# Expert loop of a mixture-of-experts kernel: outputs in two PSUM banks in turns, turned activations in one

## The chip, the core and the metric

The kernel runs on one core of a Trainium2 chip. A core has a matrix engine (TensorE, PE in the profile, with its weight loads as PEld), a vector engine (VectorE, DVE), a scalar engine (ScalarE, ACT), a general engine (GpSimd, POOL) and a queue for transfers (SyncE, SP). Results of TensorE land in PSUM, which this kernel uses as eight banks of 128 x 512 fp32. Each engine works through its own instructions in order; semaphores tie them together. The metric is the device time of one execution in microseconds (us); less is better.

## What is computed

A block of a transformer: a mixture-of-experts layer at half weight, attention, and the same mixture-of-experts layer again, on 4096 tokens of width 128. All arithmetic is fp32. The change lies in the mixture-of-experts layer, which runs twice:

```python
def _L0_ffn_ref(hidden_states, router_w, gate_w, up_w, down_w):
    B, S, H, F, E, TOPK = (4, 256, 128, 512, 8, 2)
    ...
    router_logits = x @ router_w.T
    top_vals, top_idx = jax.lax.top_k(router_logits, TOPK)
    routing_weights = jax.nn.softmax(top_vals, axis=-1)
    combine = jnp.sum(jax.nn.one_hot(top_idx, E, dtype=x.dtype) * routing_weights[..., None], axis=1)
    out = jnp.zeros_like(x)
    for e in range(E):
        g = x @ gate_w[e].T
        u = x @ up_w[e].T
        y = jax.nn.silu(g) * u @ down_w[e].T
        out = out + combine[:, e:e + 1] * y
    return out.reshape(b, s, h)

x = x + 0.5 * _L0_ffn_ref(_layernorm(x, axis=-1), ...)
x = x + _L0_attn_ref(_layernorm(x, axis=-1), L0_attn_W_qkv, L0_attn_W_out)
x = x + 0.5 * _L0_ffn_ref(_layernorm(x, axis=-1), ...)
```

## The kernel before

Three stages follow each other: `ffn` (f1), `attention`, `ffn` (f2). In `ffn` a first part normalizes the tokens, writes them to DRAM, routes them and sorts the 8192 token-expert pairs by expert into 72 blocks of 128 rows (`BLOCKS`), each block of one expert. The second part is the expert loop, the place of the change. A third part reads the results back and adds them with their weights.

In the expert loop the work for a block is spread over several iterations, so that one iteration j holds pieces of different blocks:

- POOL gathers the rows of block j+4 from DRAM (`gather`, L201, into one of four tiles `xb`), once PE has turned block j, and then scatters the output of block j-3 to DRAM (`scatter`, L593, from one of four tiles `y`), once ACT has copied it there. Both are indirect DMAs that POOL issues itself.
- PE, in this order: `turn_hidden(j-2)` turns the hidden activations of block j-2 (four transposes, L631); `turn_rows(j+1)` turns the gathered rows of block j+1 (L613); `project_down(j-3)` multiplies the turned activations of block j-3 with the down weights (L639, four matmuls in fp32, which the profile shows as eight records); `project(j)` does the gate and up projections of block j (L622 to L624, twice).
- ACT: copies the turned activations of block j-2 to `hidT` (L671), the turned rows of block j+1 to `xt` (L677), the output of block j-3 to `y` (L683), and makes silu of the gate of block j (L687).
- DVE: subtracts the rounded rows from the exact ones for block j+1 (L697) and multiplies silu with the up projection of block j into `hid` (L703).

The semaphores count blocks: `y_psum` is raised by the last matmul of `project_down`, `y_ready` by the copy L683, `hidT_psum` by the last transpose of `turn_hidden`, `hidT_ready` by the copy L671, `xlo_ready` by L697, `hid_ready` by L703. PE must not write into a bank that another engine has yet to read. Before the change gate and up have two banks each (0 to 3), the turned activations two (4 and 5), the turned rows one (6) and the outputs one (7). So `turn_hidden` of block i waits for the copy of block i-2, and `project_down` of block i for the copy of block i-1.

What sets the order: each engine's program is written out by hand in the order above, for all iterations; nothing reorders it.

Of the kernel before, what the change touches and what calls it, by code (L numbers as in the profile page):

```python
# [13 lines left out]
ACT = mybir.ActivationFunctionType  # L14
AX = mybir.AxisListType.X

P = 128
# [7 lines left out]
def wait(eng, sem, value):  # L25

    if isinstance(value, int) and value <= 0:
        return
    eng.wait_ge(sem, value)
# [14 lines left out]
def macaron(nc, x, w_qk, w_v, w_out, router_t, gate_t, up_t, down_t, rope_t, out):  # L44
# [6 lines left out]
    with ExitStack() as top:  # L51
# [23 lines left out]
        with nc.Block() as block:  # L75
# [9 lines left out]
            def _(pool):  # L85
# [9 lines left out]
                pool.wait_ge(consts, 6)  # L95

        ffn(nc, "f1", X, xn_dram, ys_dram, gate_t, up_t, down_t, router_t, ident,
            stats, mean, rstd, tmpa, tmpb, NB, E, FC, loaded, None)
        attention(nc, X, w_qk, w_v, w_out, rope_t, ident, identb, causal,
# [59 lines left out]
def ffn(nc, name, X, xn_dram, ys_dram, gate_t, up_t, down_t, router_t, ident,  # L159
# [14 lines left out]
    with ExitStack() as ctx:  # L174
        def sb(n, shape, dt=F32, ctx=ctx):
            return ctx.enter_context(nc.sbuf_tensor(f"{name}_{n}", shape, dt))

        def ps(n):
            return ctx.enter_context(nc.psum_tensor(f"{name}_{n}", [P, 512], F32))

        def sem(n):
            return ctx.enter_context(nc.semaphore(f"{name}_{n}"))
# [12 lines left out]
        bank = [ps(f"b{k}") for k in range(8)]  # L195
# [365 lines left out]
        hid = [sb(f"hid{k}", [P, F]) for k in range(2)]  # L561
        hidT = [sb(f"hidT{k}", [P, FC, P]) for k in range(2)]
        y = [sb(f"y{r}", [P, P]) for r in range(AHEAD)]
        gate_bank, up_bank, hid_bank, x_bank, y_bank = bank[0:2], bank[2:4], bank[4:6], bank[6], bank[7]

        xt_psum = sem("xt_psum2")
        xhi_ready = sem("xhi_ready")
# [5 lines left out]
        hidT_ready = sem("hidT_ready")  # L573
        y_psum = sem("y_psum")
        y_ready = sem("y_ready")
        y_out = [sem(f"y_out{r}") for r in range(AHEAD)]

        def has(j, d):

            return 0 <= j + d < BLOCKS  # L580

        def uses(j, r):

            return (j - r) // AHEAD

        with nc.Block() as block:
# [20 lines left out]
            @block.tensor  # L607
            def _(pe):
                def turn_rows(j, r):
                    pe.wait_ge(xb_in[r], 16 * uses(j, r) + 16)  # L610

                    wait(pe, xlo_ready, j)
                    pe.transpose(x_bank[:, 0:P], xb[r][:, :], ident[:, :]).then_inc(xt_psum, 1)  # L613

                def project(j, k, e):
                    pe.wait_ge(xlo_ready, j + 1)
                    wait(pe, hid_ready, j - 1)
                    hi, lo = xt[k][:, 0, :], xt[k][:, 1, :]
                    for w, o in ((gate, gate_bank[k]), (up, up_bank[k])):
                        wh = w[0][:, bass.ds(e, 1), :].rearrange("p a f -> p (a f)")  # L620
                        wl = w[1][:, bass.ds(e, 1), :].rearrange("p a f -> p (a f)")
                        pe.matmul(o[:, :], hi, wh, start=True, stop=False)  # L622
                        pe.matmul(o[:, :], hi, wl, start=False, stop=False)
                        one = pe.matmul(o[:, :], lo, wh, start=False, stop=True)  # L624
                        one.then_inc(gu_psum, 1)

                def turn_hidden(j, k):
                    pe.wait_ge(hid_ready, j + 1)
                    wait(pe, hidT_ready, j - 1)
                    for c in range(FC):  # L630
                        one = pe.transpose(hid_bank[k][:, c * P:(c + 1) * P], hid[k][:, c * P:(c + 1) * P],  # L631
                                           ident[:, :])
                    one.then_inc(hidT_psum, 1)

                def project_down(j, k, e):
                    pe.wait_ge(hidT_ready, j + 1)
                    wait(pe, y_ready, j)
                    for c in range(FC):
                        one = pe.matmul(y_bank[:, 0:P], hidT[k][:, c, :],  # L639
                                        down[:, bass.ds(e, 1), c, :].rearrange("p a d -> p (a d)"),  # L640
                                        start=(c == 0), stop=(c == FC - 1))
                    one.then_inc(y_psum, 1)

                def seven_owners(j):
                    all_seven = pe.value_load(owners[0:1, j - 3:j - 2], min_val=0, max_val=E ** 7 - 1)
                    return [all_seven // E ** d % E for d in range(7)]

                for first in range(-1, BLOCKS + 3, 4):

                    low = min(max(first, 3), BLOCKS - 4)  # L650
                    known = seven_owners(low)
                    for j in range(first, min(first + 4, BLOCKS + 3)):
                        k = j % 2
                        if has(j, -2):
                            turn_hidden(j - 2, k)
                        if has(j, 1):
                            turn_rows(j + 1, (j + 1) % AHEAD)
                        if has(j, -3):
                            project_down(j - 3, 1 - k, known[j - 3 - (low - 3)])
                        if has(j, 0):  # L660
                            project(j, k, known[j - (low - 3)])

            @block.scalar
            def _(act):
                def step(act, j, r):
                    k = r % 2
                    if has(j, -2):
                        act.wait_ge(hidT_psum, j - 1)

                        wait(act, y_psum, j - 3)  # L670
                        act.activation(hidT[k][:, :, :], hid_bank[k][:, :].rearrange("p (c q) -> p c q", q=P),  # L671
                                       ACT.Copy).then_inc(hidT_ready, 1)
                    if has(j, 1):
                        act.wait_ge(xt_psum, j + 2)

                        wait(act, gu_psum, 2 * (j - 1) + 2)
                        act.activation(xt[1 - k][:, 0, :], x_bank[:, 0:P], ACT.Copy).then_inc(xhi_ready, 1)  # L677
                    if has(j, -3):
                        act.wait_ge(y_psum, j - 2)

                        b = (r + 1) % AHEAD
                        wait(act, y_out[b], 16 * uses(j - 3, b))
                        act.activation(y[b][:, :], y_bank[:, 0:P], ACT.Copy).then_inc(y_ready, 1)  # L683
                    if has(j, 0):
                        act.wait_ge(gu_psum, 2 * j + 1)
                        wait(act, hid_ready, j - 1)
                        act.activation(silu[k][:, :], gate_bank[k][:, :], ACT.Silu).then_inc(silu_ready, 1)  # L687
                for j in range(-1, BLOCKS + 3):
                    step(act, j, j % AHEAD)
# [560 lines left out]
```

## Time and profile before

| | |
|---|---|
| time, median of 3 runs | 1488.47 us (1485.82 to 1488.49) |
| the profiled execution's own time | 1478.64 us |
| its span, first to last instruction | 1476.9 us |
| granted TensorE clock, mean | 0.931 |
| PE busy | 1288.9 us, 87% |
| DVE busy | 954.9 us, 65% |
| POOL busy | 783.7 us, 53% |
| ACT busy | 777.2 us, 53% |

How to read it: busy times are sums of instruction durations over one execution. Starts of instructions are recorded; the ends of matmuls are modelled. In a timeline a row gives the start in us, the duration in us, the engine, the line, the operation and what it writes and reads, the number of instructions merged, and in brackets how long the engine had been idle before it and what ended that. "remote" there is a release from outside the engines shown. The two expert loops lie at about 78 to 305 us and 1218 to 1444 us of the span.

### The profile page before, as it was taken

The numbers are of one execution on the slowest core, as the hardware profiler recorded it, in microseconds if no ns is written. First come the engines' busy times: TensorE is split into PE (matmuls) and PEld (weight loads), VectorE is DVE, ScalarE is ACT, GpSimd is POOL, SyncE is SP. The second block draws the span as 40 slices with busy tenths as digits, with TensorE's granted clock in tenths as the row PEclk, the third lists the DMA queues.
The fourth block names the chain that finished last, engine by engine and source line by source line (L and its number), as shares of the span: only waits on it lengthen the run. The fifth ranks groups of instructions, "written<-read, shape, count | busy, mean of one in ns | idle before, by whom it ended". The sixth has DMA issues, their size and how long they took to land. (4 is left out here: it accounts for less than half of the span.)

```text
span 1476.9 us, 26692 instructions
## 1 busy us (share of the span) xinstructions
PE 1288.9 (87%) x8212; PEld 933.0 (63%) x8212; DVE 954.9 (65%) x2000; ACT 777.2 (53%) x2213; POOL 783.7 (53%) x726
## 2 busy tenths in 40 slices
PE   7689999922699999999999999999998959999990
PEld 7378888821366666666666666666665728888880
DVE  6833333347388888888888888888886683332334
ACT  5644444432265556565555565655655645444452
POOL 0056666532266666666656666666664015666653
PEclk7889999965599999999999999999999689999996
DMA  8011111142111221111221112221110701111115
GB/s 285 4 37 42 44 42 44 42 123 86 43 44 44 51 51 44 44 44 44 55 47 44 44 44 48 53 45 44 44 44 15 229 8 38 44 42 44 44 37 178
DMA packets 86597, 86.68 MB, mean 59 GB/s; under 512 B 10560, under 2 KB 77120, under 8 KB 85952
## 3 DMA queue, kind: packets, MB, share of 16 engines
q1 hardware_dynamic: 73024, 63.99, 16.7%
q0 software_dynamic: 9216, 18.89, 4.3%
q10 hardware_dynamic: 4224, 2.10, 0.5%
q8 instruction: 74, 1.21, 0.3%
q14 instruction: 59, 0.48, 0.1%
HBM read 35.66 MB, written 15.73 MB: 35 GB/s over the span
## 5 line engine op out<-in xcount | busy, mean ns | idle before, releaser
L957 POOL TENSOR_SCALAR at_prob<-at_prob,at_rec 128x128 f32<-128x128 f32 (+3 forms) x256 | 316.3, 1240 | 282.3 <-DVE at_rec L1099 282.1
L1173 ACT ACTIVATE at_prob<-at_s,at_nb 128x128 f32<-128x128 f32 (+3 forms) x512 | 265.0, 526 | 44.3 <-DVE at_nb L1091 40.4
L703 DVE TENSOR_TENSOR f_hid<-f_b,f_silu 128x512 f32<-128x512 f32 x144 | 99.6, 692 | 257.2 <-ACT f_silu L687 131.0
L1182 ACT ACTIVATE at_probT<-at_pt 128x128 f32<-128x128 f32 (+3 forms) x256 | 105.0, 436 | 261.5 <-PE at_pt L1032 261.5
L201 POOL DMA_INDIRECT f_xb<-xn_dram,f_source x144 | 139.4, 968 | 181.8 <-DVE f_source L421 126.5
L1091 DVE TENSOR_REDUCE at_nb<-at_s 128x2 f32<-128x256 f32 (+3 forms) x256 | 208.7, 816 | 16.9 <-PE at_s L1020 16.9
L593 POOL DMA_INDIRECT ys_dram<-f_y,f_target x144 | 141.8, 985 | 135.6 <-ACT f_y L683 115.0
L1085 DVE TENSOR_TENSOR at_turned<-at_pj,at_rope 128x1024 f32<-128x1024 f32 x128 | 156.2, 1220 | 54.8 <-PE at_pj L987 49.4
L1032 PE MATMUL at_pt<-ident,at_prob 128*128 128x128 f32 x1280 | 183.8, 275 | 1.8 <-DVE at_prob L1102 1.2
L1015 PE MATMUL at_s<-at_KT,at_QT 64*128 64x128 f32 (+3 forms) x1024 | 174.7, 460 | 1.4 <-ACT at_prob L1173 1.4
L639 PE MATMUL f_b<-f_down,f_hidT 128*128 x1152 | 157.9, 280 | 20.2 <-ACT f_y L683 18.9
L951 POOL TENSOR_TENSOR at_R<-at_turned 128x512 f32<-128x512 f32 x128 | 159.3, 1264 | 15.2 <-DVE at_turned L1085 15.2
L1044 PE MATMUL at_o<-at_probT,at_V 128*64 128x512 f32 (+3 forms) x1024 | 152.0, 437 | 14.3 <-DVE at_probT L1109 14.3
L639 PEld LDWEIGHTS f_b<-f_down,f_hidT 128*128 128x128 f32 x1152 | 139.9, 191 | 34.3 <-issue 34.3
L1032 PEld LDWEIGHTS at_pt<-ident,at_prob 128*128 128x128 f32 x1280 | 140.5, 141 | 23.7 <-issue 13.0
L1044 PEld LDWEIGHTS at_o<-at_probT,at_V 128*64 128x64 f32 x1024 | 80.8, 136 | 97.0 <-issue 74.2
L1102 DVE TENSOR_SCALAR at_prob<-at_prob,at_rec 128x128 f32<-128x128 f32 (+3 forms) x256 | 129.3, 505 | 9.1
L1109 DVE COPY at_probT<-at_pt 128x128 f32<-128x128 f32 (+3 forms) x256 | 119.4, 487 | 8.9 <-PE at_pt L1032 0.9
L671 ACT ACTIVATE f_hidT<-f_b 128x512 f32<-128x512 f32 x144 | 86.5, 601 | 51.4 <-PE f_b L631 50.8
L683 ACT ACTIVATE f_y<-f_b 128x128 f32<-128x128 f32 x144 | 40.0, 278 | 138.5 <-remote 101.4
L1015 PEld LDWEIGHTS at_s<-at_KT,at_QT 64*128 64x128 f32 x1024 | 78.2, 188 | 50.1 <-issue 25.3
L1173 ACT ACTIVATION_READ_ACCUMULATOR at_prob<-at_s,at_nb 128x1 f32 x512 | 104.2, 204 | 0.0
(175 smaller groups left out, 2210.8 us busy)
## 6 DMA issues: line engine op xcount, KB each, us to landing
at_QT<-at_R SPq DMA_DIRECT2D x128, 128.0 KB, 2.4
at_KT<-at_R SPq DMA_DIRECT2D x128, 128.0 KB, 2.4
f_got<-ys_dram SPq DMA_DIRECT2D x32, 256.0 KB, 4.4
f_gate<-gate_t SPq DMA_DIRECT2D x16, 256.0 KB, 4.8
f_up<-up_t SPq DMA_DIRECT2D x16, 256.0 KB, 6.4
xn_dram<-f_xn SPq DMA_DIRECT2D x16, 256.0 KB, 4.6
f_down<-down_t SPq DMA_DIRECT2D x2, 2048.0 KB, 8.2
f_xb<-xn_dram,f_source POOLq DMA_INDIRECT x144
```

Of the source, the lines that this page charges most:

```text
L201: pool.indirect_dma_start(out=xb[j % AHEAD][:, :], out_offset=None, in_=xn_dram, in_offset=bass.IndirectOffsetOnAxis(ap=source[:, j:j + 1] ...
L593: pool.indirect_dma_start(out=ys_dram, out_offset=bass.IndirectOffsetOnAxis(ap=target[:, j:j + 1], axis=0), in_=y[k][:, :], in_offset=None ...
L639: one = pe.matmul(y_bank[:, 0:P], hidT[k][:, c, :], down[:, bass.ds(e, 1), c, :].rearrange("p a d -> p (a d)"), start=(c == 0), stop=(c == ...
L951: pool.tensor_tensor(R[:, :, cols], turned[0][:, :, cols], turned[1][:, :, cols], ALU.add).then_inc(r_ready, 1)
L957: pool.tensor_scalar(w, w, rec[:, q, 1:2], None, ALU.mult).then_inc(probB_ready, 1)
L1015: pe.matmul(s_bank[q % 2][:, h, 0:n], q_tile[rows, q * P:n], k_tile[rows, 0:n], start=True, stop=False)
L1032: one = pe.transpose(pt_bank[h][:, at:at + P], prob[q][:, h, b * P:(b + 1) * P], ident[:, :])
L1044: one = pe.matmul(o_bank[64 * h:64 * h + 64, b * P:SEQ], V[(i // 4) % 2][:, b, 128 * j + 64 * h:128 * j + 64 * h + 64], probT[h][:, b, b * ...
L1085: dve.tensor_tensor(turned[half][:, :, :], src, rope[:, half, :, :], ALU.mult).then_inc(rope_ready, 1)
L1091: dve.tensor_reduce(nb[:, q, :], s_bank[q % 2][:, :, 0:(q + 1) * P], axis=AX, op=ALU.max, negate=True).then_inc(nb_ready, 1)
L1102: dve.tensor_scalar(w, w, rec[:, q, 0:1], None, ALU.mult).then_inc(probA_ready, 1)
L1173: act.activation(prob[q][:, h, :], s_bank[q % 2][:, h, 0:n], ACT.Exp, bias=nb[:, q, h:h + 1], scale=1.0, accum_out=sums[:, q, h:h + 1]).th ...
```

## The change

The eight banks are dealt out anew: the turned activations get one bank (4) and the outputs two (5 and 7), used in turns by the parity of the block. The waits that guard the banks follow: `turn_hidden` of block i now waits for the copy of block i-1, `project_down` of block i for the copy of block i-2. The reads on ACT name the new banks. On every engine the instructions stay the same in number, kind and order.

```diff
-        gate_bank, up_bank, hid_bank, x_bank, y_bank = bank[0:2], bank[2:4], bank[4:6], bank[6], bank[7]
+        gate_bank, up_bank, hid_bank, x_bank, y_bank = bank[0:2], bank[2:4], bank[4], bank[6], (bank[5], bank[7])
...
                 def turn_hidden(j, k):
                     pe.wait_ge(hid_ready, j + 1)
-                    wait(pe, hidT_ready, j - 1)
+                    wait(pe, hidT_ready, j)
                     for c in range(FC):
-                        one = pe.transpose(hid_bank[k][:, c * P:(c + 1) * P], hid[k][:, c * P:(c + 1) * P],
+                        one = pe.transpose(hid_bank[:, c * P:(c + 1) * P], hid[k][:, c * P:(c + 1) * P],
                                            ident[:, :])
...
                 def project_down(j, k, e):
                     pe.wait_ge(hidT_ready, j + 1)
-                    wait(pe, y_ready, j)
+                    wait(pe, y_ready, j - 1)
                     for c in range(FC):
-                        one = pe.matmul(y_bank[:, 0:P], hidT[k][:, c, :],
+                        one = pe.matmul(y_bank[k][:, 0:P], hidT[k][:, c, :],
...
-                        act.activation(hidT[k][:, :, :], hid_bank[k][:, :].rearrange("p (c q) -> p c q", q=P),
+                        act.activation(hidT[k][:, :, :], hid_bank[:, :].rearrange("p (c q) -> p c q", q=P),
                                        ACT.Copy).then_inc(hidT_ready, 1)
...
-                        act.activation(y[b][:, :], y_bank[:, 0:P], ACT.Copy).then_inc(y_ready, 1)
+                        act.activation(y[b][:, :], y_bank[1 - k][:, 0:P], ACT.Copy).then_inc(y_ready, 1)
```

## Rows read from the trace of the kernel before

**Rows 1.** By stage: us, busy of PE, PEld, DVE, ACT, POOL, PEclk, DMA, GB/s

```profile
78.00:305.00 227.00, 214.36 (x1368) 184.01 (x1368) 69.78 (x144) 113.04 (x289) 135.70 (x139) 0.99 0.14 41
1218.00:1444.00 226.00, 214.34 (x1367) 184.16 (x1367) 69.66 (x144) 112.90 (x287) 135.52 (x139) 0.99 0.14 41
```

**Rows 2.** Timeline of PE early in loop 1: groups of L639, start and duration

```profile
95.05 1.06 PE L639 MATMUL f_b<-f_down,f_hidT 128*128 x8
97.89 1.06 PE L639 MATMUL f_b<-f_down,f_hidT 128*128 x8
```

**Rows 3.** Line L639 in 97.8 to 290.5 and 1237 to 1430: count, durations, starts

```profile
L639 PE MATMUL f_b<-f_down,f_hidT x496: 275/275/373, 97.9 to 290.0; 128*128 x166
...
L639 PE MATMUL f_b<-f_down,f_hidT x496: 275/275/372, 1237.2 to 1429.2; 128*128 x166
```

**Rows 4.** Waits in loops 1 and 2: us in total, times, longest

```profile
ACT f_y L683 <- remote: 50.9, 27, 2.1
...
PE f_b L639 <- ACT f_y L683: 9.6, 26, 0.6
...
PE f_b L639 <- ACT f_y L683: 9.3, 25, 0.6
```

**Rows 5.** Timeline of two blocks in the middle of loop 1

```profile
201.21 0.99 POOL L593 DMA_INDIRECT ys_dram<-f_y,f_target  x1 [1.49 <-ACT f_y L683]
...
203.77 0.99 POOL L593 DMA_INDIRECT ys_dram<-f_y,f_target  x1 [0.30 <-issue]
...
204.21 1.06 PE L639 MATMUL f_b<-f_down,f_hidT 128*128 x8
204.30 0.60 ACT L671 ACTIVATE f_hidT<-f_b 128x512 f32<-128x512 f32 x1 [0.55 <-PE f_b L631]
...
205.06 0.97 POOL L201 DMA_INDIRECT f_xb<-xn_dram,f_source  x1 [0.30 <-issue]
...
206.49 0.60 PE L631 MATMUL f_b<-ident,f_hid 128*128 128x128 f32 x4
...
206.88 0.28 ACT L683 ACTIVATE f_y<-f_b 128x128 f32<-128x128 f32 x1 [1.81 <-remote]
...
207.39 1.13 PE L639 MATMUL f_b<-f_down,f_hidT 128*128 x8 [0.19 <-ACT f_y L683]
207.43 0.98 POOL L593 DMA_INDIRECT ys_dram<-f_y,f_target  x1 [1.40 <-ACT f_y L683]
```

**Rows 6.** Timeline of the end of loop 1, where no block is left to gather

```profile
289.24 1.06 PE L639 MATMUL f_b<-f_down,f_hidT 128*128 x8
...
294.92 1.06 PE L639 MATMUL f_b<-f_down,f_hidT 128*128 x8
...
296.01 0.28 ACT L683 ACTIVATE f_y<-f_b 128x128 f32<-128x128 f32 x1 [0.24 <-PE f_b L639]
```

**Rows 7.** Timeline around the longest step of loop 1

```profile
260.54 1.06 PE L639 MATMUL f_b<-f_down,f_hidT 128*128 x8
...
261.73 0.97 POOL L201 DMA_INDIRECT f_xb<-xn_dram,f_source  x1 [0.30 <-issue]
...
262.00 0.28 ACT L683 ACTIVATE f_y<-f_b 128x128 f32<-128x128 f32 x1 [0.60 <-PE f_b L639]
...
262.82 0.60 PE L631 MATMUL f_b<-ident,f_hid 128*128 128x128 f32 x4
...
263.36 1.06 PE L639 MATMUL f_b<-f_down,f_hidT 128*128 x8
...
264.30 0.97 POOL L201 DMA_INDIRECT f_xb<-xn_dram,f_source  x1 [0.30 <-issue]
...
266.30 0.60 ACT L671 ACTIVATE f_hidT<-f_b 128x512 f32<-128x512 f32 x1 [2.98 <-PE f_b L631]
...
267.53 0.30 PE L613 MATMUL f_b<-ident,f_xb 128*128 128x128 f32 x1 [1.29 <-DVE f_xt L697]
...
267.86 0.37 PE L639 MATMUL f_b<-f_down,f_hidT 128*128 x1
```

## The prediction

> **What bounds the kernel now.** I began with the table by stage, to see what a change inside the two expert loops can reach. They take 453 of 1477 us, both at a granted clock of 0.99, with TensorE (PE) busy for 94% of it [rows 1]. That looks PE-bound, so the next question was how fast PE goes when nothing holds it. In the timeline two groups of project_down (L639), one block apart, start at 95.05 and 97.89: **2.84 us a block** [rows 2]. Then the count: from the group at 97.89 to that at 289.24 there are 496 matmul records, eight to a block, so 62 blocks and 61 steps in 191.35 us; the second loop has 496 as well, with 192.0 us from its first record to its last where the first has 192.1 [rows 2, 3, 6]. That is 3.137 us a block in both. The lost 0.297 x 122 steps = 36.2 us is all that any edit of the waits in these loops can win.
>
> Who loses it? PE waits for the copy of y (L683) 26 times for 9.6 us and 25 times for 9.3 us [rows 4]. The longer wait stands one engine further: ScalarE (ACT) sits before that same copy for 50.9 us in 27 waits put down to "remote" [rows 4]. A timeline of two blocks shows why, and it is not the bank:
> - POOL issues its DMAs in trains of four: scatter 201.21, gather, scatter 203.77, gather 205.06 [rows 5]. From the first to the last is 3.85 us, a step of 1.283.
> - PE's matmuls for y start at 204.21 and take 1.06, so they end at 205.27. The copy starts at 206.88, 1.61 later, though ACT's last work (the transposed x) is long done [rows 5]. ACT waits there for two semaphores, y_psum and the scatter four blocks back. That scatter was issued four blocks of 3.1 us earlier, so I put the delay on y_psum: PE has finished and its signal comes late.
> - The copy comes 1.82 us after the start of the gather at 205.06 [rows 5]. Without gathers, at the end of the loop, matmuls from 294.92 for 1.06 end at 295.98 and the copy starts at 296.01 [rows 6]. So I read it as this: while POOL issues a train of DMAs, PE's finished-signals are held until the last gather of the train is out.
> - The copy at 206.88 releases the next scatter at 207.43 and PE's next project_down at 207.39 [rows 5].
>
> (On PE's ends: the Trainium skill, "Perfetto Trace Analysis", section on the Tensor Engine instruction, says that the profiler's end of a matmul is estimated from its size, and the signal is pushed when PSUM acknowledges. The trace agrees with the estimate where no gather runs, 0.03 us from end to copy.)
>
> So the beat is a **loop through POOL**: three steps 3.85, last gather to copy 1.82, copy to scatter 0.55, together 6.22 us for two blocks, or 3.11 a block, against 3.137 on average. PE's work in it is 2 x 2.84 = 5.68. The 0.54 us between them, which PE loses mostly before the single y bank, is slack of this loop, not its cause.
>
> **The change, part by part.** Instructions are the same in number, kind and order on every engine; only PSUM banks and two wait values change, so no instruction's duration changes.
> 1. *project_down waits for the copy of block j-2 instead of j-1.* In the pair the group at 207.39 could follow PE's other work at once, since the copy it then needs was made a block earlier. That removes the 9.6 + 9.3 = 18.9 us of PE waits, and with the slower first matmuls behind each wait at most the 36.2 above. What is late next is POOL's train: 6.22 contains no PE work.
> 2. *turn_hidden waits for the ACT copy of the block before, not two before.* In the pair that copy (L671) starts at 204.30 and takes 0.60, done at 204.90; the next transposes start at 206.49 [rows 5]. Margin 1.59 us, or about 1.2 with PE not held: nothing. If the transposes' signal is itself held, the margin is gone: see the jam below, where it costs between 0 and 0.6 us (one copy).
> 3. *The y tiles and y_out waits* are as before: nothing.
>
> **What PE's new freedom does.** If PE gains those 0.54 us in a pair, the y matmuls that now end at 205.27, 0.21 *behind* the start of the last gather, end 0.33 ahead of it, and their signal may get out. The trace has this case once in each loop. At 260.54 the matmuls run to 261.60, ahead of the gather at 261.73; the copy comes at 262.00, only 0.40 late [rows 7]. POOL then doesn't pause: it goes on with a scatter and the gather at 264.30. Now signals are held over the longer train: the transposes that start at 262.82 for 0.60 end at 263.42, and ACT gets them at 266.30, after 2.98 us idle, 2.00 after the last gather. PE itself runs dry, since its transpose of x (L613) needs the x copy and subtraction of that held block; it starts at 267.53, and project_down goes from 263.36 to 267.86, a step of **4.50 us** [rows 7]. Two y banks don't help there: none of these waits is for y.
>
> **Forecast: slower, through jams.** With y out of the way I expect PE to run four blocks at 2.84 and then meet such a jam, again and again: after the jam the first train is again of four, the next one lets y through. Five blocks then take 4 x 2.84 + 4.50 = 15.86 us against 5 x 3.137 = 15.69, or +0.035 a block, +4.3 us over 122. The row is the mildest case, as part of its signals slipped out before the long hold. At worst the whole 2.98 us of the late signal stands in front of PE, so 2.84 + 2.98 = 5.82 for the jam, 17.18 for five, +0.299 a block, +36 us. I take 4.65, near the row: 16.01, or 3.202 a block, +0.065 x 122 = **+7.9 us**. The profiled execution would go from 1478.6 to 1486.5; it lies 9.8 below the median of the runs, 1488.5, from which I count: **1496.4 us**. This case's own range is 1491.5 to 1525.
>
> **Rivals.**
> - *Full gain.* The hold never stalls PE, as POOL may lag PE by nearly four blocks (four x tiles, four y tiles), and POOL needs only 2 x 1.283 = 2.57 us a block. Then 122 x 2.84: -36.2 us, 1452.3. For it: early in the loop blocks do follow each other at 2.84 [rows 2]. Against it: at 2.57 in 2.84 POOL's trains never end, and the jam is what long trains did. 0.17.
> - *Trains of six without a jam.* Five steps 6.42, 1.82, 0.55: 8.79 us for three blocks, 2.93 a block, -0.207 x 122 = -25 us, 1463. For it: PE's work for three blocks is 8.52. If part of the trains stay at four or the restart takes the 1.23 us of the jam (266.30 to 267.53) [rows 7], half of it: -12, 1476. Against: the one train of six in the trace jammed PE. 0.21 for this stretch.
> - *Same beat.* The trains stay at four because something else on PE takes the wait over, or the earlier signal is held too; 6.22 as before, within 3 us of 1488.5. 0.20. A rule of the Trainium skill points the same way: "TensorE: Matmul & The Clock Gate", section on HAM oscillation, reports that adding PSUM double-buffering gave no further gain (126.6 against 125.5 us) in a kernel that waited for DMA. By it the time would stay at 1488.5; no row here shows that kernel, but the 50.9 us of ACT's wait are of that kind.
> - *Slower by jams*, the forecast and the case on the other side: 0.42. It decides when y's signal gets out ahead of the last gather more often than once a loop.
> - *The change doesn't do what it says*: the waits are really relaxed by one block in the code, so I give this nothing.
>
> **How the numbers follow.** Faster by over 0.2% (about what a measurement of this kernel can tell from no change, 3 us): 0.17 + 0.21 = 0.38. Within: 0.20. Slower: 0.42. The likeliest case gives 1496.4. The range leaves out the full gain and the dearest jams: 1460 to 1512.
>
> **What would show it.** PE's wait for the y copy at L639 must vanish (now 9.6 and 9.3). The 61 steps of L639 from the fifth block on should take about 195 us a loop: below 188 the loop through POOL is not what I think, at 173 it never was. In the timeline I expect steps of 2.84 with one of 4.5 to 5 every five or so, ACT's waits for "remote" and for the transposes up, POOL's trains of six and more, and new waits on PE: L613 for the subtraction (L697) and, if the jams are dear, L631 for hid (L703). A wait of L631 for L671 would mean that the single hidden bank costs. The rest of the kernel must be unchanged. I am wrong if late signals are not bound to POOL's gathers, or if PE rides over them.

## The result, and the profile after

| | before | after |
|---|---|---|
| median of 8 runs each | 1487.18 us (1484.98 to 1488.49) | 1490.76 us (1488.43 to 1492.95) |
| ratio | | 1.0025, 95% interval 1.0014 to 1.0036 |
| the profiled execution | 1478.64 us | 1489.43 us |
| span, mean granted clock | 1476.9 us, 0.931 | 1487.7 us, 0.919 |

The change makes the kernel **slower by 3.6 us, 0.25%**. The forecast was +7.9 us (1496.4), and the case's own range began at 1491.5, just above the measured median. The two profiled executions lie 10.8 us apart, which overstates it: that of after was 1.3 us below the median of its kernel, that of before 8.5 below. At 1478.64 us it lies below all eight timed runs of its kernel (1484.98 and up), and inside what the same kernel takes on one of the chips met later (chip 9, 1477.68 to 1480.54). So the two profiles may come from two chips; the record does not name them. Differences between them are given below, but the sizes are taken from chip 9, where both kernels have a profile near their median.

The table by stage first (the kernel after; columns as in [rows 1]). The granted clock has gone from 0.99 to 0.95 in both. The busy times of PE (before 214.36 and 214.34) can't be compared one to one: the loops now run on past the end of the stretch, which holds 1345 and 1295 of their matmuls instead of 1368 and 1367.

```profile
78.00:305.00 227.00, 213.73 (x1345) 186.58 (x1345) 70.24 (x144) 111.11 (x285) 133.78 (x137) 0.95 0.14 41
1218.00:1444.00 226.00, 206.85 (x1295) 179.58 (x1296) 69.26 (x147) 107.64 (x276) 132.28 (x136) 0.95 0.14 41
```

Then the length of the loops, as the prediction took it: 61 steps between groups of L639. The timeline of PE in the kernel after has these four groups; they answer to 97.89 and 289.24 in [rows 2, 6].

```profile
98.56 1.06 PE L639 MATMUL f_b<-f_down,f_hidT 128*128 x8
...
293.35 1.06 PE L639 MATMUL f_b<-f_down,f_hidT 128*128 x8
...
1242.70 1.06 PE L639 MATMUL f_b<-f_down,f_hidT 128*128 x8
...
1439.95 1.06 PE L639 MATMUL f_b<-f_down,f_hidT 128*128 x8
```

That is 194.79 us and 197.25 us, against 191.35 and 191.18: +9.5 us between these two profiles.

The waits tell what came in place of the old one (the kernel after, loop 1, then loop 2; us in total, times, longest). L639 no longer waits for the copy of y, which was 9.6 us in 26 waits [rows 4]. ACT's waits for "remote" before that copy fell from 50.9 us to 21.1. New are 11 us a loop of L631 waiting for L671, in only five waits.

```profile
ACT f_y L683 <- remote: 21.1, 12, 2.5
ACT f_hidT L671 <- remote: 20.1, 6, 3.7
...
PE f_b L631 <- ACT f_hidT L671: 11.2, 5, 2.4
```

```profile
ACT f_hidT L671 <- remote: 21.2, 8, 3.7
...
ACT f_y L683 <- remote: 16.1, 8, 2.4
...
PE f_b L631 <- ACT f_hidT L671: 11.1, 5, 2.2
PE f_b L631 <- DVE f_hid L703: 2.1, 1, 2.1
```

One of the five, in the timeline of the kernel after (start, duration, engine, line, operation, count, idle before and its releaser):

```profile
150.12 0.39 PE L624 MATMUL f_b<-f_up,f_xt 128*128 x1
...
150.16 0.97 POOL L201 DMA_INDIRECT f_xb<-xn_dram,f_source  x1 [0.30 <-issue]
150.35 0.60 PE L631 MATMUL f_b<-ident,f_hid 128*128 128x128 f32 x4
...
150.89 1.06 PE L639 MATMUL f_b<-f_down,f_hidT 128*128 x8
151.44 0.99 POOL L593 DMA_INDIRECT ys_dram<-f_y,f_target  x1 [0.31 <-issue]
...
152.73 0.96 POOL L201 DMA_INDIRECT f_xb<-xn_dram,f_source  x1 [0.30 <-issue]
...
152.88 0.69 DVE L703 TENSOR_TENSOR f_hid<-f_b,f_silu 128x512 f32<-128x512 f32 x1 [3.63 <-PE f_b L624]
...
152.94 0.40 PE L624 MATMUL f_b<-f_up,f_xt 128*128 x1
154.95 0.60 ACT L671 ACTIVATE f_hidT<-f_b 128x512 f32<-128x512 f32 x1 [3.70 <-remote]
...
155.69 0.63 PE L631 MATMUL f_b<-ident,f_hid 128*128 128x128 f32 x4 [2.35 <-ACT f_hidT L671]
155.75 0.29 DVE L697 TENSOR_TENSOR f_xt<-f_b,f_xt 128x128 fp32r<-128x128 f32 x1 [2.18 <-ACT f_xt L677]
...
156.19 0.30 PE L613 MATMUL f_b<-ident,f_xb 128*128 128x128 f32 x1
...
156.51 2.07 PE L639 MATMUL f_b<-f_down,f_hidT 128*128 x8
...
161.03 1.06 PE L639 MATMUL f_b<-f_down,f_hidT 128*128 x8
```

- The transposes of 150.35 are over at 150.95 by their modelled end, and ACT copies them at 154.95, 4.00 later and 2.22 after the start of the gather at 152.73. POOL's DMAs run at one step of 1.28 from the scatter at 146.31 until that gather, six in a train. This is the late signal of [rows 7]. It is not held quite as the prediction says, until the last gather of the train and all at once: the signal of the up projection at 150.12, which ends at 150.51 by the model, gets out ahead of the others and lets DVE start at 152.88.
- PE runs dry for 2.35 us, until 155.69. The step from 150.89 to 156.51 takes 5.62.
- Then comes something that [rows 7] does not have. The same eight records take 2.07 instead of 1.06, and the *next* step, 156.51 to 161.03, takes 4.52. The table by stage of the same kernel shows why:

```profile
153.34:155.69 2.35, 0.00 (x1) 0.03 (x1) 0.23 (x1) 0.74 (x3) 0.36 (x1) 1.00 0.12 30
155.69:159.70 4.01, 3.98 (x17) 3.43 (x18) 1.28 (x3) 1.71 (x6) 2.48 (x3) 0.60 0.11 33
160.00:170.00 10.00, 10.00 (x70) 8.92 (x69) 3.59 (x7) 5.81 (x14) 5.92 (x7) 1.00 0.13 39
```

The granted clock was 1.00 while PE stood still, and is 0.60 over the 4 us in which it works again: most of them at the lower of its two levels (1.2 of 2.4 GHz). Then it is back at 1.00. Before, after a wait of 1.29 us, the first two groups of L639 took 1.15 and 1.06 and the clock stayed at 1.00:

```profile
265.65 0.60 PE L631 MATMUL f_b<-ident,f_hid 128*128 128x128 f32 x4
...
270.78 1.06 PE L639 MATMUL f_b<-f_down,f_hidT 128*128 x8
```

```profile
265.90:270.00 4.10, 2.79 (x18) 2.19 (x16) 1.24 (x3) 2.62 (x8) 1.95 (x2) 1.00 0.10 32
```

(Both fences are of the kernel before, the second its table by stage.)

**The books of the loops after.** Counted over the groups of L639 in both loops: 11 steps of 5.42 to 5.79 us, on average 5.56; 8 of them are followed by a step of 3.78 to 4.53, on average 4.27; four smaller ones are 3.57 to 4.09; the other steps are 2.82 to 2.95. Over 2.84 the eleven cost 29.9 us, the eight second steps 11.4, the four small ones 3.6, together 44.9 of the 45.5 us that the loops take over 122 x 2.84 = 346.5. So a stall comes about once in eight blocks and costs 3.0 us. Before, the loss was 36.0 us, most of it paid in small coin, about 0.3 in each block.

**The trains.** Counted over POOL's DMAs in both loops (a train is a run of starts at most 1.36 us apart): before there are 58 trains of four, two of five and none of six; after there are 12 of six. The eleven long steps of after all stand at the end of one of these 12, and the twelfth has a step of 4.09. The one long step in each loop of before comes behind a train of five: the row below (the kernel before) starts 1.50 behind the scatter ahead of it, with 0.52 idle instead of 0.30, and the five DMAs from there to the gather at 264.30 of [rows 7] follow at 1.28.

```profile
259.17 0.97 POOL L201 DMA_INDIRECT f_xb<-xn_dram,f_source  x1 [0.52 <-issue]
```

**Whose signal is late.** The trace of the kernel before also records when a semaphore is raised, and this settles what the prediction could only argue. In [rows 5] `y_psum` is raised at 206.85, 1.58 after the modelled end of its matmul and 0.03 before the copy. So the copy did wait for PE's signal and not for a DMA; the "remote" of the profile is PE's own signal, late. Only PE's signals are found late: before, DVE starts within 0.03 us of the end of ACT's L677 in all 81 cases where it had been idle for over 0.3 us, and POOL within 0.28 of ACT's L683 in all 80 where it had been idle for over 0.4. And they are late only in the expert loops: between POOL's last DMA of the first loop, at 305.5 us, and its next one, at 1209.5, lies attention, and there none of PE's 1002 signals comes later than 0.015 us after the modelled end. The profiles of after, e5, e6 and e7 show the same of that stretch.

Last, the end of each loop, which the prediction did not look at. The kernel before, then the kernel after, timeline of PE:

```profile
300.38 1.06 PE L639 MATMUL f_b<-f_down,f_hidT 128*128 x8
302.09 1.15 PE L639 MATMUL f_b<-f_down,f_hidT 128*128 x8 [0.22 <-issue]
303.79 1.13 PE L639 MATMUL f_b<-f_down,f_hidT 128*128 x8 [0.55 <-ACT f_y L683]
```

```profile
304.49 1.06 PE L639 MATMUL f_b<-f_down,f_hidT 128*128 x8
305.90 2.05 PE L639 MATMUL f_b<-f_down,f_hidT 128*128 x16
```

Before, the last groups stand 1.71 and 1.70 apart, each behind the copy of the one ahead. After, the last two run without a gap (sixteen records in 2.05 us). From the group that ends the 61 steps to the last of the loop it was 14.56 us and is 13.48: **-1.08 us a loop**.

### The profile page after: what moved, and what is told of

Same layout as the page of the kernel before. It is cut to its first block and busy times, and to the rows that moved or that the text cites. A ratio compares the mean times of both kernels' runs of the same rounds, so it can differ in the third digit from the quotient of the medians.

```text
span 1487.7 us, 26692 instructions
## 1 busy us (share of the span) xinstructions
PE 1294.5 (87%) x8212; PEld 942.6 (63%) x8212; DVE 955.5 (64%) x2000; ACT 777.0 (52%) x2213; POOL 783.8 (53%) x726
## 5 line engine op out<-in xcount | busy, mean ns | idle before, releaser
L703 DVE TENSOR_TENSOR f_hid<-f_b,f_silu 128x512 f32<-128x512 f32 x144 | 99.6, 692 | 229.9 <-PE f_b L624 130.6
L639 PE MATMUL f_b<-f_down,f_hidT 128*128 x1152 | 159.8, 284 | 0.4
L639 PEld LDWEIGHTS f_b<-f_down,f_hidT 128*128 128x128 f32 x1152 | 145.7, 198 | 2.9 <-issue 2.6
L671 ACT ACTIVATE f_hidT<-f_b 128x512 f32<-128x512 f32 x144 | 86.3, 599 | 100.9 <-PE f_b L631 49.2
L631 PE MATMUL f_b<-ident,f_hid 128*128 128x128 f32 x576 | 88.3, 277 | 25.5 <-ACT f_hidT L671 22.3
L687 ACT ACTIVATE f_silu<-f_b 128x512 f32<-128x512 f32 x144 | 86.8, 603 | 43.2 <-PE f_b L624 35.0
```

Of the source, the lines that this page charges most:

```text
L639: one = pe.matmul(y_bank[k][:, 0:P], hidT[k][:, c, :], down[:, bass.ds(e, 1), c, :].rearrange("p a d -> p (a d)"), start=(c == 0), stop=(c ...
```

## The experiments

The theory: POOL's trains of DMAs hold PE's finished-signals; before, that set the beat; after, PE runs free and meets long holds. The rivals: the signals are late for a reason that is not POOL's, or the single hidden bank is the cause. The runs were made on several chips (the numbers are only names). Each group of runs has its own runs of the kernel before on the same chip, and these turned out to be the main finding:

| runs | kernel before, median | PE's signals |
|---|---|---|
| main timing | 1487.18 us | late |
| chip 7: e1 to e4 | 1444.4 | on time |
| chip 9: e5 to e7 | 1479.23 | late |
| chip 4: e8 to e11 | 1444.75 | on time |
| chip 15: e12 to e15 | 1444.82 | on time |
| chip 2: e16 to e18 | 1444.75 | on time |

**The hidden bank alone** (e1, again as e9): the kernel before with one bank for the turned activations, y as it was.

```diff
-        gate_bank, up_bank, hid_bank, x_bank, y_bank = bank[0:2], bank[2:4], bank[4:6], bank[6], bank[7]
+        gate_bank, up_bank, hid_bank, x_bank, y_bank = bank[0:2], bank[2:4], bank[4], bank[6], bank[7]
...
-                    wait(pe, hidT_ready, j - 1)
+                    wait(pe, hidT_ready, j)
```

> The bank part of the change alone: one bank for the turned activations, still one bank for the outputs. If the single hidden bank carries the change's loss (rival), this kernel is slower than the one before by about 3.6 us and PE's L631 waits for L671 for some us in each loop. If the loss comes from the freedom of the outputs (theory), the beat of 6.22 us for two blocks stays, the new wait has a margin of 1.59 us in it, and only the one long step in each loop can grow: 0 to 3 us in all, most likely under 1.5, within 0.2%.

> The single hidden bank alone. On a chip with late signals: the beat of 6.22 us per two blocks as before, L631 waits for L671 at most in the one long step of each loop, time 0 to 2 us over the kernel before. If the single hidden bank were the loss of the change, 3 us or more over it. On a chip without late signals: no difference.

Measured: 1445.09 us, ratio 1.0004 (0.9995 to 1.0013), and 1444.36, ratio 1.0000 (0.9990 to 1.0009). The 61 steps take 173.24 us: PE is never held. On these chips the bank costs nothing, but they have none of the late signals in which it was to be tried. Neither of the two cases in the expectation of e1 was met.

**The bank from the gate instead** (e2, again as e8, e13, e18): two banks for y and two for the hidden activations, one for the gate.

```diff
-        gate_bank, up_bank, hid_bank, x_bank, y_bank = bank[0:2], bank[2:4], bank[4:6], bank[6], bank[7]
+        gate_bank, up_bank, hid_bank, x_bank, y_bank = (bank[0], bank[0]), bank[2:4], bank[4:6], bank[6], (bank[1], bank[7])
...
+                    wait(pe, silu_ready, j)
...
-                    wait(pe, y_ready, j)
+                    wait(pe, y_ready, j - 1)
```

> Two output banks and two hidden banks; the eighth bank comes from the gate, which gets one (project waits for silu of the block before). Theory: trains of POOL DMAs still grow until PE's signals are held and PE stalls every five to ten blocks, but the transposes (L631) go ahead as in the long step of the kernel before, so PE idles about 1.3 us instead of 2.4 and its clock does not fall: steps of 4.5 instead of 5.5 plus 4.1. About 2.5 us less for each of some 14 stalls: 1455 to 1480 us. Rival, that the single hidden bank does nothing: 1490 like the changed kernel. If the gate's new wait costs in each block, the short steps rise over 2.84.

> Two output banks, two hidden banks, one gate bank, once more, wanted on a chip with late signals. There the theory says: the transposes L631 run on in a stall as in the kernel before, PE idles 1.3 us instead of 2.4, its clock stays up, steps of 4.5 instead of 5.1 to 5.5 plus 4.2. If the stalls come as often as in the changed kernel, 7 to 15 us less than that one, so 0.3 to 0.9% under the kernel before. If instead POOL with its held signals has a fixed capacity (second theory: a DMA on POOL takes up 1.57 us in the long run whatever the order), the mean step stays at 3.13 and the time within 3 us of the kernel before. On a chip without late signals: within 0.2%, a little faster.

> Two output banks, two hidden banks, one gate bank. With late signals, theory: stalls as often as in the changed kernel, but PE idles less in each and its clock stays up, 3 us or more under the changed kernel. Theory of a fixed capacity of POOL: the mean step is the 3.13 us of the kernel before, time within 3 us of it. With signals on time: 0.1 to 0.2% faster than before, as measured twice.

> Two output banks, two hidden banks, one gate bank. With late signals: 3 us or more under the changed kernel (so at or under the kernel before) if the stalls are shorter with the second hidden bank, within 3 us of the kernel before if POOL's capacity sets the pace. With signals on time: 0.1 to 0.2% faster than before.

Measured: 1442.60, 1442.36, 1442.68 and 1442.70 us; ratios 0.9991, 0.9982, 0.9988 and 0.9985 (all intervals lie within 0.9973 and 1.0000). Four times about 2 us faster, all on chips with signals on time; the 1455 to 1480 us expected of e2 were for late ones. The steps are 2.84 there in any case, so the gain is not the beat: it is the end of the loops, 13.40 us in the trace of e2 against 14.56 in that of e1, which has the single y bank, -2.3 us in two loops. The changed kernel gains the same on such a chip (e12 below, 0.9987 beside the 0.9988 of e13).

**POOL only gathers** (e3 with the banks of after, again as e10, e14, e16; e4 with those of before). SyncE stores the outputs, one block after the other, so they land in the wrong rows: these kernels leave out the scatter and are read for time alone.

```diff
-                    pool.indirect_dma_start(
-                        out=ys_dram, out_offset=bass.IndirectOffsetOnAxis(ap=target[:, j:j + 1], axis=0),
-                        in_=y[k][:, :], in_offset=None).then_inc(y_out[k], 16)
...
+                    sp.wait_ge(y_ready, j + 1)
+                    sp.dma_start(ys_dram[j * P:(j + 1) * P, :], y[k][:, :]).then_inc(y_out[k], 16)
```

> The changed kernel without scatters on POOL: the outputs are stored in plain order by the SyncE queue, so they lie in the wrong rows. POOL issues only the gathers, one per block, with idle time between any two. Theory (trains of DMAs on POOL hold PE's signals): no train, no hold, all steps 2.84 us, both loops together some 36 to 44 us shorter than in the changed kernel, so about 1450 us. Rival (PE's signals are late for a reason of PE's own, or of the banks): the long steps stay and the time moves by less than 10 us.

> The same with the banks of the kernel before: outputs stored in plain order by SyncE, only gathers on POOL. Theory: the beat of 6.22 us is gone, y's copy follows the matmuls at once, steps of 2.84 us, and it agrees with the run of the changed banks within 0.2%: about 1450 us, which shows that the bank was not what PE lacked. Rival (the single y bank binds by itself): this one keeps steps over 2.9 and stays at least 5 us behind the other.

> The changed kernel with the outputs stored in plain order by SyncE (wrong rows), so that POOL issues one DMA a block. On a chip with late signals the theory says that they vanish with the trains: all steps 2.84 us and 36 us or more under the kernel before (2.5%), where a chip without late signals showed 0.75%. Rival (the chip is slow in signalling whatever POOL does): steps over 3 us and long ones remain.

> The changed kernel with the outputs stored in plain order by SyncE (wrong rows), POOL with one DMA a block. With late signals, theory: they vanish, all steps 2.84 us, near 1434 us as on the other chips, 45 us under the kernel before. Rival: the chip signals late whatever POOL does, steps over 3 us remain. With signals on time: 11 us under the kernel before.

> The changed kernel with the outputs stored in plain order by SyncE (wrong rows), POOL with one DMA a block. With late signals on the chip, theory: they vanish with the second DMA, all steps 2.84 us, 40 us or more under the kernel before. Rival: the chip signals late whatever POOL does, steps over 3 us remain. With signals on time: 11 us under the kernel before, as measured three times.

Measured: with the banks of after 1433.01 us (0.9925, 0.9910 to 0.9940), 1433.83 (0.9923, 0.9908 to 0.9938), 1434.28 and 1434.54 (one run each); with those of before 1437.36 (0.9947, 0.9932 to 0.9963). All have steps of 2.84 in the loop, as the full kernel has on these chips, so the 10 us lie outside the steady part and say nothing of the trains. The expectation that e3 and e4 agree within 0.2% missed: they are 4.4 us apart, 0.3%, with the same steps; 2.2 us of it are the ends of the loops (13.48 against 14.56). This was meant to be the deciding run and it never met a chip with late signals.

**Before and after once more** (e5, e6), on chip 9, where the signals are late.

> The kernel before once more, for its trace beside the others of this call. The first experiments ran at 1444 us for it instead of 1487, with PE's signals on time in the loop and every step at 2.84 us. If the late signals belong to the chip (theory), this run shows either 62 blocks at 2.84 us (time near 1444) or the beat of 3.137 (time near 1487), nothing between, and the kernels beside it show the same.

> The changed kernel beside it. Theory: where the signals are on time, the freedom of the outputs is worth only the few tenths that PE waits for y at all, 0 to 1 us, so within 0.2% of the kernel before, with no long step; where they are late, 2 to 6 us slower, with steps of 5.5 us every seven to ten blocks. Rival (the change itself makes the long steps, by the single hidden bank): long steps and a loss of 3 us or more on either.

Measured: before 1479.23 us (13 runs; the profiled one 1479.7), after 1481.92, ratio 1.0019 (1.0010 to 1.0029), +2.7 us. The expectation of e5 had 1444 or 1487 and nothing between; the beat is there, the time is 7.5 us under 1487. The 61 steps: before 190.91 and 190.44, after 192.83 and 193.21, together +4.7; the ends of the loops 14.53 and 14.56 before, 13.54 and 13.48 after, together -2.1. Sum +2.6. Over 2.84 a step the loops lose 34.9 us before and 39.6 after. Of the latter, 37.1 come in 14 stalls, with long steps of 4.22 to 5.42 us, 13 of them behind a train of six, and 5 of them with a slow step of 4.34 to 4.53 behind: once in nearly nine blocks, 2.7 us each. The waits of after in loop 1 (e6) have the same new row, and the L683 row of L639 is gone:

```profile
ACT f_hidT L671 <- remote: 15.0, 10, 3.7
...
PE f_b L631 <- ACT f_hidT L671: 7.6, 4, 2.2
...
PE f_b L631 <- DVE f_hid L703: 2.9, 2, 1.5
```

So the loss is repeated on a second chip, and by its parts.

**A brake on POOL** (e7, chip 9): the kernel after, but the scatter waits until PE has done the gate of block j as well. If long trains make long holds, shorter trains should help.

```diff
+                        if j < BLOCKS:
+                            pool.wait_ge(gu_psum, 2 * j + 1)
```

> The changed kernel with one wait more: POOL's scatter of block j-3 also waits until PE has finished the gate of block j, which is about 0.15 to 0.7 us later than it would start. This keeps POOL's DMAs in pairs with idle time behind them. Theory: where PE's signals are late behind long trains, the trains of six don't form, and some of the 36 us that the loops lose come back (5 to 30 us faster than the changed kernel); where the signals are on time, no change, within 0.2%. Rival (the hold does not depend on the length of a train): long steps as in the changed kernel, or more of them.

Measured: 1494.56 us, ratio 1.0106 (1.0089 to 1.0123) to the kernel before, and 12.6 us slower than the changed kernel, where 5 to 30 us faster were expected. The brake did not shorten the trains, it made more long ones: 26 of six and one of seven, against 13 of six in e6. In the timeline of e7 POOL makes six DMAs at one step, with only the fifth held for 0.08 more:

```profile
157.56 0.98 POOL L593 DMA_INDIRECT ys_dram<-f_y,f_target  x1 [2.24 <-ACT f_y L685]
...
162.76 0.99 POOL L593 DMA_INDIRECT ys_dram<-f_y,f_target  x1 [0.38 <-PE f_b L626]
164.05 0.97 POOL L201 DMA_INDIRECT f_xb<-xn_dram,f_source  x1 [0.30 <-issue]
167.30 0.98 POOL L593 DMA_INDIRECT ys_dram<-f_y,f_target  x1 [2.28 <-ACT f_y L685]
```

The 61 steps take 196.21 and 200.15 us, 10.3 more than in e6, and ACT's waits for "remote" before its copy to `hidT` in loop 1 go from 15.0 us in 10 to 38.4 in 16. So the expectation missed, and the run doesn't try shorter trains. With twice the long trains and more loss it speaks for the theory rather than against it, but the rival of e7 expected long steps as well, so it doesn't decide.

**A third DMA in each block** (e11, again as e15, e17): the kernel before with one more indirect gather into a tile that nobody reads, so that POOL's trains get much longer.

```diff
+                    wait(pool, spare_in, 16 * j)
+                    pool.indirect_dma_start(
+                        out=spare[:, :], out_offset=None, in_=xn_dram,
+                        in_offset=bass.IndirectOffsetOnAxis(ap=source[:, j:j + 1], axis=0)).then_inc(spare_in, 16)
```

> The kernel before with a third DMA per block on POOL: a gather of the same rows into a tile that nobody reads. POOL's issue alone then needs 3 x 1.285 = 3.86 us a block. Theory of the capacity: on a chip with late signals a block takes 3 x 1.57 = 4.7 us, in the two loops 2 x 67 x 0.85 = 114 us over what the issue alone would make it. Theory of the trains with a bounded hold: trains end only when y or x is missing, so a block takes 3.86 us plus a share of the hold (1.82 + 0.55 - 1.28 = 1.1 us once in a train of three to six), 4.0 to 4.2 us. On a chip without late signals: 3.86 us a block.

> The kernel before with a third DMA a block on POOL. With late signals: 4.7 us a block (1690 us in all) if a DMA of POOL takes 1.57 us in the long run, 4.0 to 4.3 us a block (1605 to 1640) if only the ends of trains cost. With signals on time: 1602 us as measured.

> The kernel before with a third DMA a block on POOL. With late signals: 4.7 us a block (about 1690 us) if a DMA of POOL takes 1.57 us in the long run, 4.0 to 4.3 us a block (1605 to 1640) if only the ends of trains cost. With signals on time: 1600 us as measured twice.

Measured: 1602.53, 1599.94 and 1603.58 us (before: 1444.75, 1444.82, 1444.75). A block takes 3.80 us (61 steps 231.5 us in e11), three of POOL's steps, and PE waits for gathered rows. POOL's trains are of 12 and more DMAs, up to 91 in e11. The timeline of e17 shows signals that are on time in such a train:

```profile
201.89 0.97 POOL L599 DMA_INDIRECT f_spare<-xn_dram,f_source  x1 [0.30 <-issue]
...
202.11 1.15 PE L646 MATMUL f_b<-f_down,f_hidT 128*128 x8
...
203.16 0.94 POOL L201 DMA_INDIRECT f_xb<-xn_dram,f_source  x1 [0.30 <-issue]
203.30 0.28 ACT L690 ACTIVATE f_y<-f_b 128x128 f32<-128x128 f32 x1 [0.82 <-PE f_b L646]
```

The y matmuls end at 203.26 and the copy starts 0.04 later, 0.14 after the start of a gather. On the chip of the main timing the copy of such a y came 1.82 after one [rows 5]. So back-to-back DMAs on POOL are **not enough** to hold PE's signals; the chip has to be one that does so.

**The kernel after where signals are on time** (e12, chip 15).

> The changed kernel, on whichever kind of chip this is. With signals on time: all steps 2.84 us in both, the freedom of the outputs is worth only the last steps of each loop (1.70 to 1.40 us): 1 to 2.5 us faster than before, 0.1 to 0.17%. With late signals: 2.5 to 4 us slower, with steps of 5 us every seven to ten blocks.

Measured: 1443.0 us against 1444.82, ratio 0.9987 (0.9978 to 0.9996): **faster by 1.8 us**. The timeline of e12:

```profile
150.03 1.06 PE L639 MATMUL f_b<-f_down,f_hidT 128*128 x8
...
151.12 0.28 ACT L683 ACTIVATE f_y<-f_b 128x128 f32<-128x128 f32 x1 [0.24 <-PE f_b L639]
...
151.67 0.99 POOL L593 DMA_INDIRECT ys_dram<-f_y,f_target  x1 [0.58 <-ACT f_y L683]
...
152.87 1.06 PE L639 MATMUL f_b<-f_down,f_hidT 128*128 x8
```

The copy comes 0.03 after the modelled end of the matmuls, the scatter 0.55 later, the next group after 2.84. Here POOL makes trains of two. The 61 steps take 173.24 us in both loops, as with e1 (y bank of before), and the end of a loop 13.48 instead of 14.56. The same edit gains 2 us at the loops' ends in each of the three settings (main timing, chips 9 and 15); what it does to the beat depends on the chip.

## Why the prediction was right, and where it was wrong

**The step that failed is the size, "+0.065 x 122 = +7.9 us".** It takes one jam of 4.65 us in five blocks, less the beat that it replaces, and nothing else. On chip 9, where both kernels have a profile near their median, the stalls come once in nearly nine blocks and cost 2.7 us each, not once in five at 1.81. All that the loops lose there over 2.84 a step is 39.6 us, not 24.4 x 1.81 = 44.2; less the 34.9 of the old beat that is +4.7 us, not +7.9. And the ends of the loops, which the sum had at nothing ("36.2 us is all that any edit of the waits in these loops can win"), gave -2.1. Together +2.6, and +2.7 was measured; in the main timing it was +3.6.

**Right: the direction, and the way the time is lost on such a chip.** PE's wait for the y copy was slack of another loop: the copy no longer ends a wait of L639, PE ran at 2.84, and the time came back as single long steps under late signals, behind trains of six. "The 61 steps of L639 should take about 195 us a loop": 194.79 and 197.25 in the profile of after, 192.83 and 193.21 on chip 9. The rivals of the full gain, of 2.93 a block and of the same beat did not come in on the two settings with late signals; the last could hardly be told by the time alone (1490.76 is within 3 us of its 1488.5), only by the steps. On the chips with signals on time the prediction's own sign against itself is met: "at 173 it never was", and the 61 steps take 173.24 us there with either bank. So the loop through POOL needs a chip with late signals; the kernel alone does not have it.

(The Trainium skill, "TensorE: Matmul & The Clock Gate", section on HAM oscillation, calls a second PSUM buffer without further gain where one kernel went from 126.6 to 125.5 us. The changes here, 1.0025, 1.0019 and 0.9987, are smaller than that one, so the trace agrees in size. But they are sums of a gain and a loss with causes of their own.)

**The terms of the size, one by one:**

1. *The jam* was sized at 4.65 us (+1.81) once in five blocks, after the one in [rows 7]. It measured 5.56 for the long step in 11 of 15 stalls, 8 times with a slow step behind it, +3.0 us per stall on average, but once in eight blocks. The 44.2 us stand against 44.9 measured: the two errors cancel in this profile, so the 195 us were partly luck; on chip 9 (39.6 measured) they don't. The row was the mildest case, as the prediction itself said, and it is one behind a train of five: what was called "the one train of six in the trace" has a step of 1.50 in it. From the late signal to the next L639 it is the same in both: 266.30 to 267.86 in [rows 7], 154.95 to 156.51 after, 1.56 us. What differs is how late the signal comes after the L639 ahead of it: 2.94 against 4.06.
2. *The single hidden bank* was put at nothing, and at 0 to 0.6 us in the jam. The test was named in the prediction, "a wait of L631 for L671 would mean that the single hidden bank costs", and the wait is there, 11 us a loop. But its rows show that the direct price is small: in the stall above L631 starts at 155.69 and L613 behind it at 156.19, and L613 needs the subtraction of L697, which ends at 156.04 with any number of hidden banks. That is at most 0.15 us. The step missed the **clock**: in [rows 7] PE still did transposes at 265.65 and then stood for 1.29 us; after, it stands 2.1 to 2.4 us in one piece, and 8 of 11 times the granted clock drops to its lower level behind it, which costs 11.4 us in all in the steps that follow. Whether a second hidden bank would save that can't be said from here: PE would do 0.60 us of transposes and then wait again, in the timeline above from about 154.2 (hid is there at 153.57, L703 being 152.88 plus 0.69) to 156.04, some 1.9 us, and the kernel that has both banks (e2) met no chip with late signals.
3. *The ends of the loops* had no term at all. The prediction counted only steps of 2.84, but where no projections stand between the y groups the single y bank is the bound (1.71 and 1.70 a step), and two banks save 1.08 us a loop: -2.2 us. It is in every comparison: main timing, chip 9, e12 beside e1. A timeline of the last blocks of before would have shown it.
4. *The reference for the loops.* The prediction counted its 36.2 us in an execution 8.5 us below its kernel's median, and its loops (191.35 and 191.18) are like those of chip 9 (190.91 and 190.44). What the steps of before take at 1487 us is in no profile. So the +9.5 us between the two main profiles can't be split into the change and the setting, and +9.5 - 2.2 = +7.3 is indeed more than the measured +3.6. Another 3.4 us between these profiles lie outside the loops, where the code is the same (0.7 ahead of loop 1, 2.4 between the loops, 0.3 behind loop 2).

**Left open: what holds the signals, and the share of the hidden bank.** The prediction says "while POOL issues a train of DMAs, PE's finished-signals are held". In the timelines with late signals the release comes about 2 us after the last gather's start (1.82 and 2.00 in [rows 5, 7], 2.22 above). The rival that such a chip signals late whatever runs on it is out: no signal of PE is late in the 904 us without a DMA of POOL. But e12 shows the same code without the delay, and e17 even a long train without it, so the chip has a part in it. That on a chip with late signals it is POOL's DMAs that hold them, and not something else of the expert loop that keeps time with them, is argued from these rows and not shown: the runs for it (POOL only gathering, the third DMA) went to chips without the delay each time. So did the hidden bank alone and the gate's bank, and therefore no run tells how much of the loss on such a chip is due to the single hidden bank and how much to PE's freedom; only the rows under 2 speak of it.

## What to carry to other kernels

A wait that is the slack of a longer loop may not be worth freeing: price the loop that sets the beat first, and expect the freed engine to meet the next late thing in one piece, where the clock can fall as well. When a bank changes hands, look at the loser in a stall and not in the steady beat, and at the first and last blocks apart from the middle. An effect of 0.2% is not settled by one chip: this one is 1.0025 in the main timing, 1.0019 on chip 9 and 0.9987 on chip 15. A profile whose time lies outside the timed runs of its kernel is no reference for them. If a version is to be taken from here, that of e2 is 0.9982 to 0.9991 on four chips with signals on time, no better there than the changed kernel, and untested where they are late.

## What the runs showed of the hardware

- The same single-core kernel takes 1444.4 to 1444.8 us on four chips, 1479.2 on a fifth and 1487.2 in the main timing, at about the same mean clock (0.930 for before on chip 9, 0.929 in e1 on chip 7). On chip 9 the steps hold all of the 34.6 us that it is behind the four: they take 34.9 us over 2.84 a block in 122 steps. The 8 us between 1479.2 and 1487.2 have no profile that explains them.
- Where signals are late, those that are held reach ACT 0.4 to 4.0 us after the modelled end of PE's matmuls in the rows shown; all are PE's, and all in the expert loops. In attention of the same executions PE's signals come at most 0.015 us after that end, and on the other chips ACT starts 0.03 to 0.04 us after it in the rows shown, with POOL just as busy.
- PE standing still for 1.75 to 2.35 us at full clock was followed by a slow step 13 times of 19 in the profile of after and in e6, each time with the granted clock at its lower level; over 4 us of one it is 0.60. In e7 it was one of two (1.98 us, but not 1.78). Shorter waits (0.8 to 1.6 us, in before, after, e5, e6 and e7) never were. Such a stall costs its own length and then up to 1.7 us more in the step behind it.
- Indirect DMAs of 128 rows on POOL take 0.94 to 0.99 us and follow each other at about 1.28. Three in a block bound the kernel at 3.80 us a block.
